# Unit 1's pairs 2 and 3 selected between the gram chunks of unit 0

## The chip, the cores and the metric

The kernel runs on one core of a Trainium2 chip. The metric is the device time of one execution in microseconds (us); lower is better. Three executions of the kernel before took 456.87, 457.18 and 457.71 us, median 457.18.

## What is computed

A recommendation tower over a batch of 2048 samples. Each sample looks up one 64-float row in each of 32 tables; all inner products of two different rows (496 of them), with 16 dense features behind them, go through three layers:

```python
e = jnp.stack([tbl_0[ids[:, 0]], ..., tbl_31[ids[:, 31]]], axis=1)   # 2048 x 32 x 64
gram = jnp.einsum('bnd,bmd->bnm', e, e)
z = gram[:, rows, cols]                                              # upper triangle
h = jnp.concatenate([z.reshape(2048, -1), dense_ctx], axis=1)        # 2048 x 512
h = jnp.maximum(h @ W_top1 + b_top1, 0.0)
h = jnp.maximum(h @ W_top2 + b_top2, 0.0)
y = h @ W_top3
```

All is in float32. Tables have 1000, 1250, 12500 or 125000 rows.

## The kernel before

The batch is cut into four units of 512 samples (u = 0 to 3). Each engine has one stream of instructions, written out by hand; streams meet at semaphores.

Twelve tables are *gathered*: GpSimd (POOL) issues an indirect DMA for 128 samples of one table (L272, 48 a unit), with 3 or 6 tiny memsets (L268) between two of them to pace them; the table `CLOSE` (L45) says for which numbers of a unit's 48 the pace is 3, and at the first number of that range POOL waits until TensorE has used a given piece of one-hots (L283, L284). TensorE transposes what came (L506, `turn`, three a round, two rounds r a unit) into `gat_ps`, and ScalarE (ACT) copies it to `vecs` (L314).

Twenty tables, in ten pairs g = 0 to 9, are *selected* by a matmul instead. The table lies in SBUF as three bf16 parts, 8 chunks of 125 rows (10 in pairs 7 to 9). VectorE (DVE) compares the ids of 512 samples, spread over all partitions in `ids_wide`, with row numbers (L443) and so makes one-hot columns; a pair has two halves of two pieces, and the ring `onehot` holds four pieces. `select(u, g, parts)` (L478 to L498) multiplies table parts with one-hots: 24 matmuls of 512 columns for half a pair of 8 chunks, 30 of 10 chunks. The two tables of a pair fill the upper and lower 64 partitions of one PSUM bank, `sel_ps[:, n % 2, :]`, where n numbers the pairs through all units. ACT empties it into `vecs` by four copies (`selected`, L301 to L308), and the next but one pair waits for that (L481).

The grams are matmuls of 64x32 on `vecs` (L521), in float32, recorded as two each. A unit has two rounds of four chunks; `gram(u, r, c)` is 128 recorded matmuls and 128 weight loads. Two chunks fill `gram_ps`, whose buffer b = 0 and b = 1 ACT (L323) and, for the last of a unit, DVE (L450) copy out before it is filled again (L516). `vecs` has room for one unit: ACT doesn't empty a pair of unit u + 1 before the last gram of unit u has ended (L403, L404).

SyncE then writes the grams to HBM (`rows_out`) and reads them back in the layout of the layers (`rows_back`), and TensorE does the layers of unit u - 1 between the grams of unit u, in the two banks of `tower_ps` (L537, L547, L556). At the grams of unit 0 there are no layers yet, and `tower_ps` isn't used.

TensorE's order around unit 0's grams (L572 to L586) is: half a pair 0 of unit 1, chunk (0,0,0), the other half, chunk (0,0,1), two turns, chunk (0,0,2), a turn, chunk (0,0,3), half of pair 1, chunk (0,1,0), the other half, chunks (0,1,1) to (0,1,3); then unit 1's pairs 2 to 9 (L564), each with both halves at once, and a turn behind each of the last three. DVE makes unit 1's one-hots in order, and copies the last grams of unit 0 behind those of pair 2 (L471, L472).

Of the kernel before, what the change touches and what calls it, by code (L numbers as in the profile page):

```python
# [17 lines left out]
HALF = UNIT // 2  # L18
# [23 lines left out]

SPACERS, WIDE_SPACERS = 3, 6

CLOSE = [range(0, 48), range(18, 46), range(22, 48), range(22, 48)]  # L45


def sel_no(u, g):
    return N_PAIRS * u + g
# [20 lines left out]
def dlrm_tower_kernel(nc, chunks, ctx_t, ids_gat, ids_sel, tables, packed, w1, b1, w2, b2, w3, out):  # L70
# [7 lines left out]
    with ExitStack() as ctx:  # L78
# [73 lines left out]
        y_full = sem("y_full")  # L152
        y_ready = sem("y_ready")
        y_out = [sem(f"y_out{b}") for b in range(2)]

        block = ctx.enter_context(nc.Block())

# [94 lines left out]
        @block.gpsimd  # L252
        def _(pool):
            nc.gpsimd.memset(ident[:], 0.0).then_inc(ident_zero, 1)
            for c, t in row_ids.items():
                nc.gpsimd.iota(t[:], pattern=[[1, c]], base=0, channel_multiplier=c,
                               allow_small_or_imprecise_dtypes=True).then_inc(row_ids_ready, 1)
            pool.wait_ge(ident_zero, 1)
            nc.gpsimd.affine_select(out=ident[:], in_=ident[:], compare_op=ALU.not_equal, fill=1.0, base=0,
                                    pattern=[[-1, P]], channel_multiplier=1).then_inc(ident_ready, 1)  # L260

            count = itertools.count()

            def spacer():
                n = next(count)
                if n > 0:
                    pool.wait_ge(spaced, n)
                nc.gpsimd.memset(spare[:], 0.0).then_inc(spaced, 1)  # L268

            def gather(u, r, x, k, h):  # L270
                at = ((u * ROUNDS + r) * 2 + h) * N_GAT + k
                nc.gpsimd.indirect_dma_start(  # L272
                    out=rows[:, r, k, h, :], out_offset=None, in_=tables[GATHERED[k]],
                    in_offset=bass.IndirectOffsetOnAxis(ap=gat_ids[:, at:at + 1], axis=0)).then_inc(rows_in[r][x], 16)

            for u in range(UNITS):
                if u < 2:
                    pool.wait_ge(gat_ids_in[u], 16)
                of_unit = [(r, x, k, h) for r in range(ROUNDS) for x in range(N_TURNS) for k in GROUPS[x] for h in range(2)]
                for n, (r, x, k, h) in enumerate(of_unit):  # L280
                    if u > 0 and k == GROUPS[x].start and h == 0:
                        pool.wait_ge(gat_full, gat_no(u - 1, r, x) + 1)
                    if n > 0 and n == CLOSE[u].start:  # L283
                        pool.wait_ge(onehot_used, piece_no(u, 2, 0, 1) + 1)  # L284
                    gather(u, r, x, k, h)
                    for _ in range(SPACERS if n in CLOSE[u] else WIDE_SPACERS):
                        spacer()

        @block.scalar
        def _(act):  # L290
# [10 lines left out]
            def selected(u, g):  # L301

                act.wait_ge(onehot_used, piece_no(u, g, 1, 1) + 1)
                for at in range(2):
                    for h in range(2):
                        last = nc.scalar.copy(vecs[DIM * h:DIM * h + DIM, :, N_GAT + 2 * g + at],  # L306
                                              sel_ps[DIM * at:DIM * at + DIM, sel_no(u, g) % 2, HALF * h:HALF * h + HALF])
                last.then_inc(sel_emptied, 1)  # L308

            def gathered(u, r, x):  # L310
# [105 lines left out]
        @block.vector  # L416
        def _(dve):
            dve.wait_ge(sel_ids_in, 16)
            nc.vector.tensor_copy(sel_f16[:], sel_ids[:]).then_inc(sel_f16_ready, 1)
            dve.wait_ge(row_ids_ready, len(row_ids))  # L420

            def rest(g):
                dve.wait_ge(hi_ready, g + 1)
                c0, k = pair_chunks[g]
                piece = stage[g % STAGE_SLOTS][:, 0:k, :]
                nc.vector.tensor_tensor(piece, piece, tabs[:, c0:c0 + k, 0, :], ALU.subtract).then_inc(rest_ready, 1)  # L426

            def low(g):
                dve.wait_ge(mid_ready, g + 1)
                c0, k = pair_chunks[g]  # L430
                nc.vector.tensor_tensor(tabs[:, c0:c0 + k, 2, :], stage[g % STAGE_SLOTS][:, 0:k, :],  # L431
                                        tabs[:, c0:c0 + k, 1, :], ALU.subtract).then_inc(tabs_ready, 1)

            def one_hots(u, g, half):
                if half == 0:
                    dve.wait_ge(wide_in[g], 16 * (u + 1))
                for at in range(2):
                    k, n = 2 * g + at, piece_no(u, g, half, at)
                    if n >= RING:
                        dve.wait_ge(onehot_used, n - RING + 1)  # L440
                    c0, c1 = halves[k][half]
                    for c in range(c0, c1):
                        last = nc.vector.tensor_scalar(onehot[:, n % RING, c - c0, :], ids_wide[:, k, :],  # L443
                                                       row_ids[chunks[k]][:, c:c + 1], None, ALU.is_equal)
                    last.then_inc(onehot_ready, 1)

            def gram(u, r, b, halves):
                dve.wait_ge(gram_full, emptied_no(u, r, b) + 1)
                for h in halves:
                    nc.vector.tensor_copy(gram_rows[:, r, h, :, 16 * b:16 * b + 16],  # L450
                                          gram_ps[:, h, :, :].rearrange("p i m -> p m i")).then_inc(gram_emptied, 1)

            rest(0)
            low(0)
            one_hots(0, 0, 0)
            rest(1)
            one_hots(0, 0, 1)
            low(1)
            rest(2)
            for g in range(1, N_PAIRS):  # L460
                one_hots(0, g, 0)
                if g + 1 < N_PAIRS:
                    low(g + 1)
                one_hots(0, g, 1)
                if g + 2 < N_PAIRS:
                    rest(g + 2)
            for u in range(1, UNITS):
                for g in range(N_PAIRS):
                    one_hots(u, g, 0)
                    one_hots(u, g, 1)  # L470
                    if g == 2:  # L471
                        gram(u - 1, 1, 1, (0, 1))  # L472
            for b in range(2):
                gram(LAST, 1, b, (1,))

        @block.tensor
        def _(pe):
            def select(u, g, parts=(0, 1)):  # L478
                n = sel_no(u, g)
                if n >= 2 and parts[0] == 0:  # L480
                    pe.wait_ge(sel_emptied, n - 1)  # L481
                if u == 0:
                    pe.wait_ge(tabs_ready, g + 1)
                last = [None, None]
                for half in parts:
                    pe.wait_ge(onehot_ready, piece_no(u, g, half, 1) + 1)
                    c0, c1 = halves[2 * g][half]
                    for c in range(c0, c1):
                        for part in range(PARTS):
                            for at in range(2):  # L490
                                k = 2 * g + at
                                last[at] = nc.tensor.matmul(  # L492
                                    sel_ps[DIM * at:DIM * at + DIM, n % 2, :], tabs[:, first_chunk[k] + c, part, :],
                                    onehot[:, piece_no(u, g, half, at) % RING, c - c0, :],
                                    start=(c == 0 and part == 0), stop=(c == chunks[k] - 1 and part == PARTS - 1),
                                    skip_group_check=True)
                    for at in range(2):
                        last[at].then_inc(onehot_used, 1)  # L498
# [62 lines left out]
            select(0, 1)  # L561
            pe.wait_ge(ident_ready, 1)
            for u in range(UNITS):
                for g in range(2, N_PAIRS):  # L564
                    select(u, g)
                    if g == 2 and u > 1:
                        layer3(u - 2)
# [1 line left out]
                        turn(u, 0, g - N_PAIRS + N_TURNS)  # L569
                if u == 0:  # L570

                    select(1, 0, (0,))  # L572
                    gram(0, 0, 0)
                    select(1, 0, (1,))
                    gram(0, 0, 1)
                    turn(0, 1, 0)
                    turn(0, 1, 1)
                    gram(0, 0, 2)
                    for x in range(2, N_TURNS):
                        turn(0, 1, x)  # L580
                    gram(0, 0, 3)
                    select(1, 1, (0,))
                    gram(0, 1, 0)
                    select(1, 1, (1,))
                    for c in range(1, CHUNKS):
                        gram(0, 1, c)  # L586
                    pe.wait_ge(w_in, 16 * 5)
                elif u < LAST:
# [94 lines left out]
```

## Time and profile before

| | |
|---|---|
| median of three executions | 457.18 us |
| profiled execution | 458.73 us |
| its span, first to last instruction | 456.9 us |
| TensorE matmul (PE) busy | 396.5 us, 87% |
| VectorE (DVE) busy | 231.5 us, 51% |
| ScalarE (ACT) busy | 166.6 us, 36% |
| GpSimd (POOL) busy | 303.5 us, 66% |
| mean granted TensorE clock | 0.978 |

Start times in rows are microseconds from the start of the span. An end of a matmul is modelled, so that two groups in a row overlap by some 0.07 us; distances are best taken from start to start. "issue" as the releaser of an idle time means that nothing else in the profile explains it. The granted clock is a share of 2.4 GHz: 1.00 is 2.4 GHz and 0.50 is 1.2 GHz.

### The profile page before, as it was taken

How to read it: one execution, taken by the hardware profiler on the slowest of the kernel's cores; microseconds unless marked ns; L12 is line 12 of the kernel's file. 1: busy time of each engine (PE TensorE's matmuls, PEld its weight loads, DVE VectorE, ACT ScalarE, POOL GpSimd, SP SyncE). 2: the span in 40 equal slices, each digit the busy share in tenths (PEclk: the TensorE clock that was granted, in tenths of full speed). 3: DMA queues.
4: the chain of work that ended last, by engine and by line, in shares of the span. 5: the costliest groups of instructions: out<-in, count | busy, mean ns of one | idle time of the engine just before them, and what ended most of it. 6: DMA issues, size and time to landing. Idle time of an engine off the chain costs nothing.

```text
span 456.9 us, 15285 instructions
## 1 busy us (share of the span) xinstructions
PE 396.5 (87%) x6516; PEld 224.8 (49%) x6516; DVE 231.5 (51%) x717; ACT 166.6 (36%) x264; POOL 303.5 (66%) x968
## 2 busy tenths in 40 slices
PE   0777788978679999789889999979999999888998
PEld 0343344554445555445544655445554655454476
DVE  2999999732239887004327897203517896000000
ACT  3346755511044435122144443312154433421222
POOL 6888889887848898778738888778608886000000
PEclk9999999997769999999999999999999999999999
DMA  5944912101056921100037832010027510024610
GB/s 179 379 129 110 322 43 61 45 19 22 18 101 128 252 64 45 20 20 16 19 51 157 236 81 65 19 21 18 14 43 151 117 23 19 3 31 78 118 51 0
DMA packets 38238, 37.53 MB, mean 82 GB/s; under 512 B 13781, under 2 KB 26903, under 8 KB 38042
## 3 DMA queue, kind: packets, MB, share of 16 engines
q1 hardware_dynamic: 31594, 29.04, 25.4%
q0 software_dynamic: 6144, 6.30, 6.7%
q10 hardware_dynamic: 432, 1.21, 0.8%
q8 instruction: 51, 0.84, 0.8%
q14 instruction: 17, 0.14, 0.1%
HBM read 28.45 MB, written 8.09 MB: 80 GB/s over the span
## 4 chain that ended last, share of the span: by engine, by line
PE 75%; DVE 12%; issue 7%; ACT 3%; DMA 2%; ACTq 0%
PE sel_ps L492 42%; PE tower_ps L537 12%; PE gram_ps L521 12%; DVE onehot L443 8%; PE tower_ps L547 5%; PE gat_ps L506 2%; DVE tabs L431 2%; ACT vecs L306 2%; DVE work L426 2%; PE tower_ps L556 2%; DMA ids_wide<-ids_scratch 1%; DMA ids_scratch<-sel_f 1%; ACT work L323 1%; DMA sel_ids<-in_ids_sel_dram 1%; ACT tabs L299 0%
## 5 line engine op out<-in xcount | busy, mean ns | idle before, releaser
L492 PE MATMUL sel_ps<-onehot,tabs 128*64 128x512 bf16 x2064 | 237.6, 387 | 32.3 <-DVE onehot L443 15.1
L443 DVE TENSOR_SCALAR onehot<-ids_wide,row_ids 128x512 bf16<-128x512 f16 x688 | 202.7, 366 | 123.7 <-PE sel_ps L492 115.1
L272 POOL DMA_INDIRECT rows<-in_tbl_dram,gat_ids x192 | 195.3, 1017 | 48.0 <-PE sel_ps L492 26.2
L492 PEld LDWEIGHTS sel_ps<-onehot,tabs 128*64 128x64 bf16 x2064 | 125.3, 112 | 139.0 <-issue 40.1
L306 ACT COPY vecs<-sel_ps 64x256 f32<-64x256 f32 x160 | 96.9, 605 | 112.2 <-PE sel_ps L492 69.3
L268 POOL MEMSET spare<- 128x1 f32 x768 | 107.8, 140 | 33.2
L521 PE MATMUL gram_ps<-vecs 64*32 64x32 f32 x4096 | 54.3, 204 | 24.9 <-issue 22.6
L521 PEld LDWEIGHTS gram_ps<-vecs 64*32 64x32 f32 x4096 | 44.9, 108 | 50.0 <-issue 45.6
L537 PE MATMUL tower_ps<-work,w_sb 128*128 128x512 f32 (+1 forms) x160 | 59.3, 515 | 0.5 <-issue 0.5
L537 PEld LDWEIGHTS tower_ps<-work,w_sb 128*128 128x128 f32 x160 | 29.0, 190 | 19.0 <-issue 17.0
L450 DVE COPY work<-gram_ps 128x512 f32<-128x512 f32 x8 | 5.3, 688 | 61.5 <-PE gram_ps L521 61.5
L323 ACT COPY work<-gram_ps 128x512 f32<-128x512 f32 x24 | 13.0, 589 | 55.0 <-PE gram_ps L521 55.0
L329 ACT ACTIVATE h<-tower_ps,b_sb 128x512 f32<-128x512 f32 (+1 forms) x20 | 12.0, 602 | 57.1 <-PE tower_ps L537 57.1
L547 PE MATMUL tower_ps<-h,w_sb 128*128 128x512 f32 (+1 forms) x80 | 29.7, 516 | 0.0
L299 ACT CAST tabs<-work 128x1024 bf16<-128x1024 f32 (+1 forms) x10 | 11.1, 1109 | 25.3 <-DVE work L426 19.6
L547 PEld LDWEIGHTS tower_ps<-h,w_sb 128*128 128x128 f32 x80 | 14.6, 190 | 9.2 <-issue 8.1
L314 ACT COPY vecs<-gat_ps 128x512 f32<-128x512 f32 x24 | 13.8, 594 | 13.2 <-PE gat_ps L506 12.9
L506 PE MATMUL gat_ps<-ident,rows 128*128 128x128 f32 x96 | 14.9, 284 | 0.8 <-ACT vecs L314 0.8
L426 DVE TENSOR_TENSOR work<-work,tabs 128x1024 f32<-128x1024 f32 (+1 forms) x10 | 12.9, 1292 | 2.5 <-ACT tabs L294 2.5
L506 PEld LDWEIGHTS gat_ps<-ident,rows 128*128 128x128 f32 x96 | 10.1, 140 | 7.0 <-issue 5.8
L431 DVE TENSOR_TENSOR tabs<-work,tabs 128x1024 bf16<-128x1024 f32 (+1 forms) x10 | 12.9, 1294 | 1.1 <-ACT tabs L299 1.1
L294 ACT CAST tabs<-work 128x1024 bf16<-128x1024 f32 (+1 forms) x10 | 11.1, 1108 | 5.3 <-DMA work<-in_packed_dram 5.1
(13 smaller groups left out, 20.3 us busy)
## 6 DMA issues: line engine op xcount, KB each, us to landing
ids_wide<-ids_scratch SPq DMA_DIRECT2D x40, 256.0 KB
rows<-in_tbl_dram,gat_ids POOLq DMA_INDIRECT x192
products<-work SPq DMA_DIRECT2D x12, 248.0 KB
products<-work SPq DMA_DIRECT2D x24, 120.0 KB
work<-in_packed_dram SPq DMA_DIRECT2D x5, 512.0 KB
work<-products SPq DMA_DIRECT2D x9, 256.0 KB
work<-in_packed_dram SPq DMA_DIRECT2D x3, 640.0 KB
work<-in_packed_dram ACTq DMA_DIRECT2D x2, 512.0 KB
```

The lines of the kernel that those rows point to most:

```text
L268: nc.gpsimd.memset(spare[:], 0.0).then_inc(spaced, 1)
L272: nc.gpsimd.indirect_dma_start(out=rows[:, r, k, h, :], out_offset=None, in_=tables[GATHERED[k]], in_offset=bass.IndirectOffsetOnAxis(ap=g ...
L306: last = nc.scalar.copy(vecs[DIM * h:DIM * h + DIM, :, N_GAT + 2 * g + at], sel_ps[DIM * at:DIM * at + DIM, sel_no(u, g) % 2, HALF * h:HAL ...
L323: nc.scalar.copy(gram_rows[:, r, h, :, 16 * b:16 * b + 16], gram_ps[:, h, :, :].rearrange("p i m -> p m i")).then_inc(gram_emptied, 1)
L426: nc.vector.tensor_tensor(piece, piece, tabs[:, c0:c0 + k, 0, :], ALU.subtract).then_inc(rest_ready, 1)
L431: nc.vector.tensor_tensor(tabs[:, c0:c0 + k, 2, :], stage[g % STAGE_SLOTS][:, 0:k, :], tabs[:, c0:c0 + k, 1, :], ALU.subtract).then_inc(ta ...
L443: last = nc.vector.tensor_scalar(onehot[:, n % RING, c - c0, :], ids_wide[:, k, :], row_ids[chunks[k]][:, c:c + 1], None, ALU.is_equal)
L492: last[at] = nc.tensor.matmul(sel_ps[DIM * at:DIM * at + DIM, n % 2, :], tabs[:, first_chunk[k] + c, part, :], onehot[:, piece_no(u, g, ha ...
L506: last = nc.tensor.transpose(gat_ps[:, n % 2, P * at:P * at + P], rows[:, r, k, :, :].rearrange("p h d -> p (h d)"), ident[:])
L521: last = nc.tensor.matmul(gram_ps[32 * s:32 * s + 32, h, i, :], v, v, start=True, stop=True, skip_group_check=True)
L537: last = nc.tensor.matmul(tower_ps[:, (v + j) % 2, 0:width], w1_sb[:, c, P * j:P * j + P], z[:, c, x0:x0 + width], start=(c == 0), stop=(c ...
L547: last = nc.tensor.matmul(tower_ps[:, (v + o) % 2, 0:width], w2_sb[:, j, P * o:P * o + P], h1[:, j, 0:width], start=(j == 0), stop=(j == J ...
```

## The change

Pairs 2 and 3 of unit 1 are put into the two banks of `tower_ps` and moved in front of the chunks of round 1. TensorE's order at unit 0's grams becomes eight times half a pair (pairs 0 to 3 of unit 1) and a chunk, with two turns in front of the third half and one in front of the fourth; the loop of unit 1 then begins with pair 4. The waits of `select` follow: pairs 2 and 3 wait for no emptying, and pairs 4 and 5 for that of pairs 0 and 1, which is what pairs 2 and 3 waited for. DVE copies the last grams of unit 0 between the two halves of pair 4's one-hots. `CLOSE` changes for units 1 to 3, and POOL's wait in unit 1 is for pair 4 instead of pair 2.

```diff
-CLOSE = [range(0, 48), range(18, 46), range(22, 48), range(22, 48)]
+CLOSE = [range(0, 48), range(18, 42), range(17, 45), range(20, 48)]
@@
+        def sel_bank(u, g):
+
+            return tower_ps[:, g - 2, :] if u == 1 and g in (2, 3) else sel_ps[:, sel_no(u, g) % 2, :]
@@ POOL
-                        pool.wait_ge(onehot_used, piece_no(u, 2, 0, 1) + 1)
+                        pool.wait_ge(onehot_used, piece_no(u, 4 if u == 1 else 2, 0, 1) + 1)
@@ ACT, selected
-                                              sel_ps[DIM * at:DIM * at + DIM, sel_no(u, g) % 2, HALF * h:HALF * h + HALF])
+                                              sel_bank(u, g)[DIM * at:DIM * at + DIM, HALF * h:HALF * h + HALF])
@@ DVE
                     one_hots(u, g, 0)
+                    if u == 1 and g == 4:
+                        gram(0, 1, 1, (0, 1))
                     one_hots(u, g, 1)
-                    if g == 2:
+                    if u > 1 and g == 2:
                         gram(u - 1, 1, 1, (0, 1))
@@ TensorE, select
-                if n >= 2 and parts[0] == 0:
+                if u == 1 and g in (4, 5) and parts[0] == 0:
+                    pe.wait_ge(sel_emptied, n - 3)
+                elif n >= 2 and parts[0] == 0 and not (u == 1 and g in (2, 3)):
                     pe.wait_ge(sel_emptied, n - 1)
@@
-                                    sel_ps[DIM * at:DIM * at + DIM, n % 2, :], tabs[:, first_chunk[k] + c, part, :],
+                                    sel_bank(u, g)[DIM * at:DIM * at + DIM, :], tabs[:, first_chunk[k] + c, part, :],
@@ TensorE, order
-                for g in range(2, N_PAIRS):
+                for g in range(4 if u == 1 else 2, N_PAIRS):
@@
-                    select(1, 0, (0,))
-                    gram(0, 0, 0)
-                    select(1, 0, (1,))
-                    gram(0, 0, 1)
-                    turn(0, 1, 0)
-                    turn(0, 1, 1)
-                    gram(0, 0, 2)
-                    for x in range(2, N_TURNS):
-                        turn(0, 1, x)
-                    gram(0, 0, 3)
-                    select(1, 1, (0,))
-                    gram(0, 1, 0)
-                    select(1, 1, (1,))
-                    for c in range(1, CHUNKS):
+                    for c in range(CHUNKS):
+                        if c == 2:
+                            turn(0, 1, 0)
+                            turn(0, 1, 1)
+                        if c == 3:
+                            turn(0, 1, 2)
+                        select(1, c // 2, (c % 2,))
+                        gram(0, 0, c)
+                    for c in range(CHUNKS):
+                        select(1, 2 + c // 2, (c % 2,))
                         gram(0, 1, c)
```

## Rows read from the trace of the kernel before

**Rows 1.** The page: the chain that ended last, shares by engine.
```profile
PE 75%; DVE 12%; issue 7%; ACT 3%; DMA 2%; ACTq 0%
```

**Rows 2.** Stretches: PE, PEld, DVE, ACT, POOL busy, granted clock, DMA share, GB/s.
```profile
110.00:120.00 10.00, 7.53 (x357) 5.00 (x353) 4.73 (x16) 1.07 (x2) 8.30 (x33) 1.00 0.09 16
...
150.00:160.00 10.00, 9.51 (x88) 5.74 (x86) 9.08 (x32) 4.28 (x8) 8.95 (x25) 1.00 0.88 253
```

**Rows 3.** Timeline of TensorE: start, length, what, idle before. Unit 0's grams.
```profile
92.85 2.78 PE L492 MATMUL sel_ps<-onehot,tabs 128*64 128x512 bf16 x24
...
97.29 1.09 PE L506 MATMUL gat_ps<-ident,rows 128*128 128x128 f32 x8
...
101.63 0.66 PE L506 MATMUL gat_ps<-ident,rows 128*128 128x128 f32 x4
...
106.40 4.50 PE L492 MATMUL sel_ps<-onehot,tabs 128*64 128x512 bf16 x24
...
113.39 2.78 PE L492 MATMUL sel_ps<-onehot,tabs 128*64 128x512 bf16 x24
...
117.25 0.94 PE L521 MATMUL gram_ps<-vecs 64*32 64x32 f32 x84 [0.45 <-issue]
...
119.36 1.11 PE L521 MATMUL gram_ps<-vecs 64*32 64x32 f32 x90 [1.17 <-ACT work L323]
```

**Rows 4.** Timeline of TensorE behind unit 0's grams.
```profile
128.52 18.60 PE L492 MATMUL sel_ps<-onehot,tabs 128*64 128x512 bf16 x144 [2.49 <-issue]
147.38 10.71 PE L492 MATMUL sel_ps<-onehot,tabs 128*64 128x512 bf16 x96 [0.26 <-issue]
...
180.03 3.60 PE L537 MATMUL tower_ps<-work,w_sb 128*128 128x512 f32 x8
```

**Rows 5.** Stretches of one us: TensorE busy, granted clock, DMA share, GB/s.
```profile
103.00:104.00 1.00, 0.97 (x51) 0.51 0.18 33
...
120.00:121.00 1.00, 0.47 (x45) 0.54 0.17 33
...
133.00:134.00 1.00, 1.00 (x8) 0.63 0.81 141
...
404.00:405.00 1.00, 0.32 (x37) 1.00 0.00 0
```

**Rows 6.** Timeline of TensorE: half pairs and chunks of units 1 and 2.
```profile
213.79 2.78 PE L492 MATMUL sel_ps<-onehot,tabs 128*64 128x512 bf16 x24
...
218.28 2.78 PE L492 MATMUL sel_ps<-onehot,tabs 128*64 128x512 bf16 x24
...
223.56 3.70 PE L547 MATMUL tower_ps<-h,w_sb 128*128 128x512 f32 x8
...
319.25 2.78 PE L492 MATMUL sel_ps<-onehot,tabs 128*64 128x512 bf16 x24
...
323.62 2.78 PE L492 MATMUL sel_ps<-onehot,tabs 128*64 128x512 bf16 x24
...
328.16 3.70 PE L547 MATMUL tower_ps<-h,w_sb 128*128 128x512 f32 x8
```

**Rows 7.** Timeline of TensorE: a chunk of unit 1 between two parts of layer 1.
```profile
203.44 0.69 PE L521 MATMUL gram_ps<-vecs 64*32 64x32 f32 x44
...
206.88 1.09 PE L506 MATMUL gat_ps<-ident,rows 128*128 128x128 f32 x8
```

**Rows 8.** Timelines of ACT, DVE, POOL and SyncE's queue behind unit 0's grams.
```profile
126.06 4.74 ACT L306 COPY vecs<-sel_ps 64x256 f32<-64x256 f32 x8 [6.76 <-PE gram_ps L521]
126.07 1.29 DVE L450 COPY work<-gram_ps 128x512 f32<-128x512 f32 x2 [7.46 <-PE gram_ps L521]
...
133.93 2.33 DVE L443 TENSOR_SCALAR onehot<-ids_wide,row_ids 128x512 bf16<-128x512 f16 x8 [6.57 <-PE sel_ps L492]
...
134.13 0.97 POOL L272 DMA_INDIRECT rows<-in_tbl_dram,gat_ids  x1 [5.85 <-PE sel_ps L492]
...
148.34 0.43 SPq L201 DMA_DIRECT2D work<-products  x1
```

## The prediction

> **What bounds the kernel now.** I began with the page's chain of waits, by engine. The reader should see that three quarters of the span are TensorE [rows 1], so a change counts only by what it does to TensorE's stream. Then came TensorE's timeline at unit 0's grams, which is read by start-to-start distances. Half a pair takes 2.7 us, and it is followed by a chunk. From 92.85 to 97.29 a half and a chunk together take 4.44 us; from 113.39 to 118.19 (the end of the chunk's last piece, 117.25 + 0.94) 4.80 us [rows 3]. Chunks with another chunk or turns in front are dearer. From 97.29 to 106.40 lie three turns and two chunks: 9.11 us, of which the turns are 1.09 + 0.66 us, so a chunk costs 3.7 us. The last two chunks run from 119.36 [rows 3] to 126.06, where ACT is released [rows 8]: 3.35 us each, and 1.17 us of waiting for ACT lie ahead of them. The idle times inside the chunks have no releaser but "issue". Between such pauses 90 matmuls run in 1.11 us [rows 3]. So a chunk is not limited by the array; it is limited by how fast instructions reach it, and a chunk behind long matmuls has part of its instructions waiting in TensorE's queue already.
>
> The granted clock gives the second loss. It falls to 0.50 (1.2 GHz) in the us from 103, and again in the us from 120, both times when nothing but chunks, turns and idle time had come since the last half pair; it is back in the us from 133 [rows 5]. The half pair at 106.40 takes 4.50 us where the others take 2.78 [rows 3].
>
> The third loss is the wait behind the last chunk: TensorE idles until 128.52 [rows 4], since pair 2 needs the bank of pair 0, and ACT may empty that only when unit 0's last gram has ended; its eight copies for two pairs take 4.74 us, so one pair 2.4 us [rows 8].
>
> **The change part by part.** Up to 97.29 both kernels issue the same.
>
> *Eight halves before eight chunks.* From 97.29 come three turns, 1.09 + 0.66 = 1.75 us [rows 3], and six times a half with a chunk. This combination at full clock is seen six times apart from the first: 4.44 and 4.80 [rows 3], and in units 1 and 2 213.79 to 218.28 = 4.49, 218.28 to 223.56 = 5.28, 319.25 to 323.62 = 4.37, 323.62 to 328.16 = 4.54 [rows 6]. The mean is 27.92 / 6 = 4.65 us. So the last gram ends at 97.29 + 1.75 + 27.9 = 126.9, and not at 126.06: 0.9 us later, with 96 more matmuls done. Lower bound: all at 4.37, 125.3. Upper bound: all at 5.28, 130.7. I take the mean, since half of the six lie within 0.15 us of it.
>
> *The wait behind the grams stays.* Pair 4 needs pair 0's bank as pair 2 did, so TensorE waits 2.5 us again and starts pair 4 at 126.9 + 2.5 = 129.4.
>
> *Where the old kernel stands at the same point.* Its pairs 2, 3 and 4 are the 144 matmuls from 128.52, ending at 147.12; a pair at full clock is 5.36 us, half of the 10.71 us of 96 matmuls [rows 4]. It begins pair 4 at 147.12 - 5.36 = 141.8. The gain is 141.8 - 129.4 = **12.4 us**. In other terms: 1.7 us for the half pair at 1.2 GHz, 2.6 us for the time from 128.52 to 133.7 at 1.2 GHz (half of 5.2), and 8.1 us of issue time and of the wait for ACT that long matmuls now cover.
>
> *The other bank.* No row shows a selection into `tower_ps`. Layers write it, 8 recorded matmuls in 3.70 us [rows 6] with no idle time ahead that the bank caused, and ACT empties it behind them; I take 0. As bounds: a gain is excluded, as nothing gets shorter; the loss is at most what an ordinary wait for ACT costs here, 1.2 us [rows 3].
>
> *ACT's copies.* Four pairs now wait for the last gram. At 2.4 to 2.5 us a pair ACT is through at 126.9 + 9.9 = 136.8 and through with pair 4 at 139.3. Pair 6 needs that at 129.4 + 2 x 5.36 = 140.1. The cover is 0.8 us; gone, it costs up to 1 us once, as ACT is twice as fast per pair as TensorE. ACT's program is otherwise unmoved, so the layers' copies aren't queued behind anything new.
>
> *DVE's copy of the last grams* sits between the halves of pair 4's one-hots. Behind it is queued the second half: 126.9 + 1.29 + 2.4 = 130.6 [rows 8], wanted at 129.4 + 2.7 = 132.1. The next half starts when the first of pair 4 is used, 132.1, and is there at 134.5, wanted at 134.8. During the grams DVE makes a half in 2.33 us [rows 8], of the 4.65 that TensorE needs. Cost 0; if the cover of 0.3 us is gone, some tenths, as in the old trace, whose idle 0.26 us ahead of 147.38 [rows 4] is of this kind.
>
> *SyncE* sends unit 0's grams out when both copies are done, now 0.9 us later, and then reads them back; the last read was issued at 148.34 [rows 8], and the DMA engines were 0.88 busy from 150 to 160 [rows 2]. Layer 1 started at 180.03 [rows 4] and will want the data at 167.7. With the issue at 149.2 that leaves 18 us. Cost 0; the bounds are below as a rival. The loads of `ids_wide` behind it wait for one-hots, which come earlier too.
>
> *POOL.* Its gather 18 of unit 1 waited until 134.13 for pair 2 [rows 8] and now waits for pair 4's first half, 129.4 + 2.7 = 132.1: 2 us earlier, while TensorE is 12.4 us ahead. The last turns of unit 1 come at some 201; 30 gathers, each 1.0 us [rows 8] and at most as much again for its memsets, end by 192 at most. `CLOSE` keeps the dense gathers to the stretch without layers. Cost and gain both within 0.5 us, taken as 0.
>
> From there on all is moved as a whole. The profiled execution, 458.73 us with its span of 456.9, becomes 446.3, and as it lies 1.6 us above the median of 457.18, the median becomes **444.8 us**.
>
> **A rule of the notes, weighed.** 90 of a chunk's matmuls in 1.11 us [rows 3] are 12 ns each. The Trainium skill, "TensorE: Matmul & The Clock Gate", section "Wait — 56ns, not 53.3ns?", says that matmuls never start closer than about 25 ns, however small. By that a chunk would be 3.2 us whatever stands in front of it. The trace disagrees; but chunks of about that length exist here, and so the matter is a rival, below, with its own rows.
>
> **Rivals.**
> - *The clock falls once more, in the wait behind the last chunk.* For: from the end of the last half pair to pair 4 lie a chunk (about 1.9 us) and 2.5 us of idleness, 4.4 us without long matmuls, and the fall in the us from 120 came some 4 us after the half pair from 113.39. Against: in unit 3, in the us from 404, TensorE is 0.32 busy between two parts of a layer, and the clock stays at 1.00 [rows 5]; a fall so late hits little. Price: 1.7 us (one half pair at 4.50 for 2.78) to 2.6 us (the second time). Result 446.5 to 447.4, say 447.1.
> - *A chunk has its own price.* In unit 1 the chunk from 203.44 to 206.88 takes 3.44 us [rows 7] though 3.6 us of layer 1 stand ahead of it. If chunks cost 3.2 us here, each of the six pairs is 2.7 + 3.2 = 5.9 us, 1.25 more than taken, together 7.5: 452.3. Against: no chunk behind a half pair at full clock took over 2.6 us.
> - *The products come back late.* If rows written 0.9 us later landed only at 175, layer 1 would start 7.3 us after TensorE is ready: 452.1; landing as late as 180 leaves nothing. Against: the DMA share of the ten us from 150 [rows 2] is the reading back itself.
> - *Slower than before.* The clock goes to 1.2 GHz at 103 as it did and never gets back between the halves, since chunks leave TensorE idle now and then. Then six halves cost 1.72 more, 10.3 us, the six chunks about 0.4 more, 2.4, and pair 4 2.6: 444.8 + 15.3 = 460.1. It decides if half of a stretch isn't enough to keep the clock. Against: from 110 to 120 TensorE did a chunk, a half pair and a chunk, 7.53 us busy of ten, and the clock stayed at 1.00 [rows 2].
>
> **How the numbers follow.** The forecast has 0.56, the clock's fall behind the grams 0.27, the chunk's own price 0.07, late products 0.04, slower 0.03, and something not seen that eats the gain 0.03. The lower end is the six combinations at 4.37: 444.8 - 1.7 = 443.1, rounded to 442.8. Upwards the combinations at 5.28 give 448.6, and a fall of the clock with combinations a little above the mean 450; the rivals at 452 and above stay out. A difference under 0.2% (0.9 us) can't be told from none here. Faster by more: 0.94; within: 0.02; slower: 0.04.
>
> **What will show it.** In the trace of the changed kernel: six half-and-chunk distances of 4.4 to 5.3 us and a last gram near 127; the clock at 1.00 from 97 to 127; an idle time of 2.5 us with ACT as its cause ahead of pair 4, at 129.4; the first part of layer 1 at 167.7 with no idle time ahead; and from there the same distances as before. I am wrong if the distances are near 6, if the clock is at 0.50 for longer than 5 us, or if an idle time stands ahead of layer 1 or pair 6.

## The result and the profile after

The changed kernel took 451.75 us (median of 454.50, 450.27, 453.06 and 450.44) against 457.44 us; the ratio is 0.9871, with a 95% interval of 0.9835 to 0.9907. It is 5.7 us faster where 12.4 were forecast, and outside the range by 1.75 us. Its profiled execution is the slowest of the four, 454.5 us with a span of 452.7, against 458.73 and 456.9 before.

At the change itself the timeline of TensorE answers to [rows 3] and [rows 4] as follows (start, length, what, idle time before it).

```profile
97.39 1.09 PE L514 MATMUL gat_ps<-ident,rows 128*128 128x128 f32 x8
98.41 2.78 PE L500 MATMUL sel_ps<-onehot,tabs 128*64 128x512 bf16 x24
...
104.30 2.78 PE L500 MATMUL sel_ps<-onehot,tabs 128*64 128x512 bf16 x24
...
108.29 2.78 PE L500 MATMUL tower_ps<-onehot,tabs 128*64 128x512 bf16 x24
...
112.66 2.78 PE L500 MATMUL tower_ps<-onehot,tabs 128*64 128x512 bf16 x24
...
117.18 2.78 PE L500 MATMUL tower_ps<-onehot,tabs 128*64 128x512 bf16 x24
...
121.64 2.78 PE L500 MATMUL tower_ps<-onehot,tabs 128*64 128x512 bf16 x24
...
127.28 0.35 PE L529 MATMUL gram_ps<-vecs 64*32 64x32 f32 x12 [0.48 <-issue]
130.15 17.74 PE L500 MATMUL sel_ps<-onehot,tabs 128*64 128x512 bf16 x144 [2.52 <-issue]
148.67 6.67 PE L500 MATMUL sel_ps<-onehot,tabs 128*64 128x512 bf16 x60 [0.78 <-DVE onehot L447]
...
170.12 3.60 PE L545 MATMUL tower_ps<-work,w_sb 128*128 128x512 f32 x8
```

The rows show six halves; each with its chunk takes 3.99 to 5.99 us. A half of a pair in `tower_ps` takes as long as one in `sel_ps` (2.78 us). The last gram ends at 127.63, the idle 2.5 us stayed, and layer 1 begins at 170.12 with nothing ahead of it. Against [rows 4] (180.03) the lead there is 9.9 us. The 144 matmuls of pairs 4 to 6 take 17.74 us where 16.1 would be full speed (three times 5.36).

Behind that point the rows of layer 1 and of the turns in units 1 and 2 tell where the lead went.

```profile
184.69 5.40 PE L545 MATMUL tower_ps<-work,w_sb 128*128 128x512 f32 x8
...
192.64 3.70 PE L545 MATMUL tower_ps<-work,w_sb 128*128 128x512 f32 x8
...
280.81 1.35 PE L529 MATMUL gram_ps<-vecs 64*32 64x32 f32 x112
...
283.66 5.40 PE L545 MATMUL tower_ps<-work,w_sb 128*128 128x512 f32 x8
...
301.37 0.64 PE L529 MATMUL gram_ps<-vecs 64*32 64x32 f32 x50
...
305.45 1.97 PE L514 MATMUL gat_ps<-ident,rows 128*128 128x128 f32 x8
307.35 7.27 PE L500 MATMUL sel_ps<-onehot,tabs 128*64 128x512 bf16 x48
...
386.78 1.88 PE L545 MATMUL tower_ps<-work,w_sb 128*128 128x512 f32 x4
```

The last of them, layer 1 at the grams of unit 3, stood in the kernel before at:

```profile
389.79 1.88 PE L537 MATMUL tower_ps<-work,w_sb 128*128 128x512 f32 x4
```

So the lead of 9.9 us is down to 3.0 there. And the stretches of 2 us (length, TensorE busy, granted clock, DMA share, GB/s) show what the clock did.

```profile
184.00:186.00 2.00, 1.54 (x8) 0.74 0.07 16
...
284.00:286.00 2.00, 2.00 (x3) 0.50 0.09 15
...
306.00:308.00 2.00, 2.00 (x11) 0.50 0.08 16
```

Three times in units 1 and 2 the clock goes to 1.2 GHz. A part of layer 1 takes 5.40 us instead of 3.70, twice; in the third stretch two turns take 1.97 instead of 1.09 and the next pair (48 matmuls) 7.27 instead of 5.37. That is 1.7 + 1.7 + 0.9 + 1.9 = 6.2 us, and 9.9 - 6.2 = 3.7; the span is 4.2 us shorter. Up to unit 3 the lead shrinks by 6.9 us, so the falls are most of it. Single chunks are up to 1.5 us longer or shorter than in the kernel before, which nearly cancels, and one half, at 319.07, takes 3.39 us at full clock. In the profile of the kernel before the clock is never below 1.00 in these units.

### The profile page after: what moved, and what is told of

Same layout as the page of the kernel before. It is cut to its first block, busy times and chain, and to the rows that moved or that the text cites. A ratio compares the mean times of both kernels' runs of the same rounds, so it can differ in the third digit from the quotient of the medians.

```text
span 452.7 us, 15283 instructions
## 1 busy us (share of the span) xinstructions
PE 398.1 (88%) x6516; PEld 223.7 (49%) x6516; DVE 230.6 (51%) x717; ACT 166.9 (37%) x264; POOL 304.6 (67%) x968
## 4 chain that ended last, share of the span: by engine, by line
PE 75%; DVE 14%; issue 6%; ACT 3%; DMA 2%; DVEq 0%
PE sel_ps L500 38%; PE tower_ps L545 13%; PE gram_ps L529 11%; DVE onehot L447 10%; PE tower_ps L555 6%; PE gat_ps L514 3%; PE tower_ps L500 2%; DVE tabs L435 2%; ACT vecs L310 2%; DVE work L430 2%; PE tower_ps L564 2%; DMA ids_wide<-ids_scratch 1%; DMA ids_scratch<-sel_f 1%; DMA sel_ids<-in_ids_sel_dram 1%; ACT tabs L303 0%
## 5 line engine op out<-in xcount | busy, mean ns | idle before, releaser
L500 PE MATMUL sel_ps<-onehot,tabs 128*64 128x512 bf16 x1968 | 226.7, 386 | 32.4 <-DVE onehot L447 16.7
L500 PEld LDWEIGHTS sel_ps<-onehot,tabs 128*64 128x64 bf16 x1968 | 118.8, 111 | 135.0 <-issue 39.7
L272 POOL MEMSET spare<- 128x1 f32 x768 | 109.1, 142 | 33.2
L310 ACT COPY vecs<-sel_ps 64x256 f32<-64x256 f32 x152 | 92.1, 606 | 103.1 <-PE sel_ps L500 60.1
L529 PE MATMUL gram_ps<-vecs 64*32 64x32 f32 x4096 | 51.8, 201 | 19.5 <-issue 18.6
L529 PEld LDWEIGHTS gram_ps<-vecs 64*32 64x32 f32 x4096 | 43.3, 105 | 44.7 <-issue 42.0
L545 PE MATMUL tower_ps<-work,w_sb 128*128 128x512 f32 (+1 forms) x160 | 62.8, 539 | 0.0
L545 PEld LDWEIGHTS tower_ps<-work,w_sb 128*128 128x128 f32 x160 | 30.1, 197 | 20.9 <-issue 18.8
```

Of the source, the lines that this page charges most:

```text
L500: last[at] = nc.tensor.matmul(sel_bank(u, g)[DIM * at:DIM * at + DIM, :], tabs[:, first_chunk[k] + c, part, :], onehot[:, piece_no(u, g, h ...
L529: last = nc.tensor.matmul(gram_ps[32 * s:32 * s + 32, h, i, :], v, v, start=True, stop=True, skip_group_check=True)
L545: last = nc.tensor.matmul(tower_ps[:, (v + j) % 2, 0:width], w1_sb[:, c, P * j:P * j + P], z[:, c, x0:x0 + width], start=(c == 0), stop=(c ...
```

## Experiments

The sessions differ. In some, a chunk behind a part of layer 1 takes 2.5 to 4.4 us; I call that slow feed. In others it takes 1.2 to 1.8; fast feed. The name is a reading: the pauses in the chunks have no releaser but "issue". It is no fixed trait of a chip: the chip with number 1 showed fast feed in one session and slow feed in another. The expectations, written as this came out, speak of chips of a first kind (slow feed) and of a second (fast feed). Every kernel is compared with the kernel before in its own session.

| kernel | time | before | ratio (95%) | feed |
|---|---|---|---|---|
| changed (first result) | 451.75 | 457.44 | 0.9871 (0.9835 to 0.9907) | slow |
| fill22 | 433.17 | 439.42 | 0.9859 (0.9827 to 0.9890) | fast |
| shift15 | 434.09 | 439.42 | 0.9892 (0.9853 to 0.9931) | fast |
| close_old | 432.70 | 439.42 | 0.9858 (0.9825 to 0.9892) | fast |
| split | 435.58 | 439.42 | 0.9921 (0.9886 to 0.9956) | fast |
| after_again (changed) | 432.00 | 438.53 | 0.9848 (0.9817 to 0.9878) | fast |
| before_again | 438.96 | 438.53 | 1.0013 (0.9992 to 1.0034) | fast |
| before_shift15 | 442.03 | 438.53 | 1.0085 (1.0058 to 1.0113) | fast |
| before_split | 442.34 | 438.53 | 1.0083 (1.0057 to 1.0108) | fast |
| before_slow | 496.69 | 456.76 | 1.0847 (1.0787 to 1.0908) | slow |
| after_slow | 493.99 | 456.76 | 1.0794 (1.0727 to 1.0861) | slow |
| gat_bank | 447.98 | 456.76 | 0.9805 (0.9753 to 0.9857) | slow |
| round0 | 457.11 | 456.76 | 0.9996 (0.9964 to 1.0028) | slow |
| after3 (changed) | 430.15 | 437.83 | 0.9845 (0.9804 to 0.9886) | fast |
| before3 | 438.76 | 437.83 | 1.0014 (0.9989 to 1.0039) | fast |
| gat_bank2 | 426.54 | 437.83 | 0.9740 (0.9717 to 0.9764) | fast |
| split2 | 436.45 | 437.83 | 0.9963 (0.9938 to 0.9987) | fast |
| after4 (changed) | 450.74 | 455.82 | 0.9893 (0.9863 to 0.9923) | slow |
| gat_bank3 | 446.36 | 455.82 | 0.9801 (0.9769 to 0.9832) | slow |

**fill22: something to do in the wait**

```diff
                     pe.wait_ge(w_in, 16 * 5)
+                    filler(22)
```

> The changed kernel with 22 matmuls of half a pair's shape, whose result nobody uses, put behind unit 0's last gram, where TensorE otherwise idles 2.5 us for ACT. Theory 1 (the lead is eaten by falls of the clock): the fall at 130 goes, layer 1 of unit 0 starts 1.7 us earlier than 170.1, at 168.4; the total is 1.7 us less if the later falls stay, and anything from 446 to 452 if they move. Theory 2 (the lead is eaten by gathers and DMA, through the new pace of POOL): layer 1 at 168.4 and the total back at what it was, 450 to 453, with the clock as it was in units 1 and 2.

The 22 matmuls are 64 x 512 and go into the first bank of `gat_ps`, where nobody reads them.

The fall behind the grams went: pairs 4 to 6 took 16.08 us and layer 1 began at 167.32, 1.8 us before close_old's 169.12 in that session. The total was no better: 433.17 us against close_old's 432.70. Its profile has a pause of 1.40 us ahead of 204.41 and a fall of the clock there, where a part of layer 2 takes 5.39 us for 3.70, and the layer parts from 211 to 223 come 1.8 to 1.9 us later than in close_old. So the local part was right, and in the profiled execution the 1.8 us and as much again were lost in the next unit. But the fall isn't the whole reason: two of the four executions have a mean clock of 1.000, so no fall, and took 432.63 and 432.93 us, no less than close_old's two at 0.996 (431.45 and 432.41). What eats the gain there isn't shown; the changed kernel itself wasn't run in that session.

**shift15 and before_shift15: everything later by 1.7 us**

```diff
+                    if u == 1 and g == 5:
+                        filler(15)
                     select(u, g)
```

> The changed kernel with 15 unused matmuls (1.7 us at full clock) in front of pair 5 of unit 1: everything behind comes 1.7 us later, nothing else differs. Theory 1: the falls of the clock in units 1 and 2 depend on when a chunk comes, so they are others than before; the total differs from +1.7 us by over 1.5 us in either direction (it may even fall to 449). Theory 2 or a fixed cost: 1.7 us more than the changed kernel, 453.4, with the falls moved along by 1.7 us.

> The kernel before with 15 unused matmuls (1.7 us at full clock) in front of pair 5 of unit 1. Theory 1: the time moves by something else than 1.7 us, as the falls of the clock move: 437 to 443. A fixed cost: 441.1.

shift15 was 1.4 us above close_old in its session, which doesn't tell the theories apart; before_shift15 was 3.5 us above the kernel before, twice the 1.7 put in. So in the second case the shift is not passed on one to one; the profiles, of one execution each, don't show why. Inconclusive.

**close_old: POOL's pace as before**

```diff
-CLOSE = [range(0, 48), range(18, 42), range(17, 45), range(20, 48)]
+CLOSE = [range(0, 48), range(18, 46), range(22, 48), range(22, 48)]
```

> The changed kernel with the table CLOSE of the kernel before, so POOL's pace is as before (its wait in unit 1 stays at pair 4). Theory 1: as the changed kernel, 450 to 454. Theory 2 (the new pace costs the lead): 445 to 447.

The ratio, 0.9858, is that of the changed kernel with fast feed (0.9848, 0.9845). With fast feed the pace table is worth nothing either way, and theory 2 is out there. With slow feed, where the lead was lost, it wasn't run.

**after_again and before_again: both kernels, one session**

> The changed kernel unaltered, on the chip of the experiments so far, where the kernel before took 439.4 us instead of 457.4. There the other kernels' chunks behind long matmuls took 1.3 to 1.8 us. Theory 4 (the size of the gain depends on how fast instructions reach TensorE on the chip at hand): the kernel before gains less from interleaving here; the changed one takes 433 to 435 us, a gain of 4.5 to 6 us. Theory 1 alone (clock falls ate it): the changed kernel's runs with a mean clock of 0.996 and above are 10 us or more ahead of the kernel before.

> The kernel before, profiled on this chip. Theory 4: chunks between two parts of layer 1 take 1.3 to 1.9 us instead of 2.6 to 3.9, in all units, which is most of the 18 us between the two chips; chunks behind chunks take about 2.5 instead of 3.3. Theory 1 alone: the same chunk times as on the first chip and only fewer falls of the clock (at most 5 us of the 18).

The rows of unit 1 in before_again, which answer to [rows 7]:

```profile
184.15 1.85 PE L521 MATMUL gram_ps<-vecs 64*32 64x32 f32 x128
185.92 3.70 PE L537 MATMUL tower_ps<-work,w_sb 128*128 128x512 f32 x8
189.56 1.29 PE L521 MATMUL gram_ps<-vecs 64*32 64x32 f32 x128
190.78 3.70 PE L537 MATMUL tower_ps<-work,w_sb 128*128 128x512 f32 x8
```

The chunks are 1.29 to 1.85 us with no pause in them. The kernel's gram rows (busy time, mean, idle time ahead), the first of the kernel before's own profile, the second of before_again, tell the same: TensorE idled 22.6 us of "issue" ahead of grams in the whole span with slow feed, and 9.2 here.

```profile
L521 PE MATMUL gram_ps<-vecs 64*32 64x32 f32 x4096 | 54.3, 204 | 24.9 <-issue 22.6 <-ACT work L323 1.4 <-ACT vecs L306 0.9
...
L521 PE MATMUL gram_ps<-vecs 64*32 64x32 f32 x4096 | 47.2, 202 | 12.2 <-issue 9.2 <-ACT work L323 1.4 <-ACT vecs L306 0.9
```

Busy and idle time of these rows together are 79.2 and 59.4 us; the difference of 19.8 is nearly all of the 20.4 us between the two spans.

The change gains 6.5 us here, a little over the 4.5 to 6 expected, and it keeps it: layer 1 begins at 169.48 against 175.71 (6.2 us), and the spans are 430.1 and 436.5 (6.4 us). Neither profile has a fall in units 1 and 2. So there is a smaller lead, nothing of it lost, and no smaller gain in the end (6.5 us; 5.7 with slow feed). The changed kernel still has the fall behind the grams: 18.69 us for the 144 matmuls, 2.6 too many.

**split, before_split, split2: half chunks between half parts of layer 1**

```diff
-                        layer1(u - 1, c)
-                        gram(u, 0, c)
+                        for part in range(2):
+                            layer1(u - 1, c, (part,))
+                            gram(u, 0, c, (part,))
```

> The changed kernel with each part of layer 1 and each chunk of round 0 of units 1 and 2 cut in two and alternated (half a layer part, half a chunk, twice). Theory 1: TensorE is never long without heavy matmuls there, the clock stays at 1.00 in units 1 and 2; and with a full queue ahead of each half chunk the distance from one layer part to the next falls from 6.6 us to 5.3, eight times: 438 to 443. Theory 3 (a chunk has a time of its own): the distances stay, and at most the falls go: 446 to 449.

> The kernel before with layer 1 and the chunks of round 0 of units 1 and 2 cut in halves and alternated. Theory 4: on this chip there is little left to gain, as whole chunks are fed fast already: 437 to 440. Theory 1: it keeps the clock up in units 1 and 2: 435 to 437.

> The changed kernel with layer 1 and the chunks of round 0 of units 1 and 2 cut in halves and alternated, on the same chip as the changed kernel. On a chip of the first kind, if slow feeding and the falls in it cost there: 3 to 8 us faster than the changed kernel, no fall between 165 and 200. On one of the second kind: 2 to 4 us slower, since a half chunk takes 0.7 us more than half of a whole one and there is nothing to save.

All three missed or were worse than hoped: split is 2.9 us slower than close_old in its session, before_split 3.8 us slower than the kernel before, split2 6.3 us slower than the changed kernel (after3). In split, the stretch from the first part of layer 1 to the turns behind the last chunk is 169.60 to 191.72, 22.1 us, where after_again needs 169.48 to 189.87, 20.4. The first half chunk waits 0.93 us for ACT, which half a part no longer hides, and a half chunk takes 0.76 us and up. All three sessions had fast feed, so what splitting does with slow feed was not seen.

**before_slow and after_slow: feeding made slower by hand**

```diff
                     for h in range(2):
+                        pe.wait_ge(ident_ready, 1)
+                        pe.wait_ge(tabs_ready, 1)
                         for s in range(Q):
```

> The kernel before with two waits that are long fulfilled ahead of every four gram matmuls (16 times a chunk): the same work, but instructions reach TensorE more slowly, as on the first chip. Theory 5 (slow feeding of the chunks makes stretches with few matmuls, in which the clock falls, and the place of the falls is a lottery): chunks between parts of layer 1 take 2.5 us or more, the time rises by over 8 us, and falls of the clock appear outside unit 0's grams. Rival (the first chip is slower for another reason, such as DMA): the time rises only by what the waits cost, all clocks as before.

> The changed kernel with the same waits in its chunks. Theory 5: with chunks as dear as on the first chip the local lead at layer 1 of unit 0 is some 10 us, more than the 6.2 us of this chip, and part of it is lost or not by falls of the clock in units 1 and 2: 4 to 11 us faster than before_slow, with runs that scatter by over 2 us. Rival: 6.5 us faster, as without the waits.

The waits cost far more than meant: 39.9 us. In before_slow's profile the granted clock is below 1.00 in seven places from 195 us on, of which two stand here (columns as in the stretches above); the kernel before's own profile has none there. Its mean fell to 0.942.

```profile
196.00:198.00 2.00, 2.00 (x4) 0.50 0.10 16
...
354.00:356.00 2.00, 2.00 (x4) 0.50 0.00 0
```

So starving TensorE of gram instructions does bring the clock down in later units, for either kernel. The change was worth 2.7 us, and its lead at layer 1 was 4.9 us (182.56 against 187.48); theory 5 gave 10 for the lead and 4 to 11 for the total, and missed both. One reading, not tested, is that waits inside a chunk are not covered by long matmuls ahead of it. At this size the waits are no copy of slow feed.

**round0: half of the change**

```diff
+                    for c in range(CHUNKS):        # turns as in the changed kernel
+                        select(1, c // 2, (c % 2,))
+                        gram(0, 0, c)
+                    for c in range(CHUNKS):
+                        gram(0, 1, c)
```

> Half of the change: the four halves of pairs 0 and 1 ahead of the four chunks of round 0, as in the changed kernel; round 1's four chunks follow each other, and pairs 2 and 3 come behind ACT's wait as before. By my prediction each half moved covers its part, so about half of the gain. By the trace of the kernel before on this chip, chunks in a row with no long matmuls lose the clock: four in a row then lose more than the three before did, and the time is that of the kernel before, 437 to 440. So the gain hangs on pairs 2 and 3 and their banks.

457.11 against 456.76: nothing. Its timeline shows why. Round 1's chunks wait for ACT's copies (1.98 and 2.42 us), the clock falls at 112 and stays down to 133, and the wait ahead of pair 2 is there.

```profile
110.35 0.58 PE L521 MATMUL gram_ps<-vecs 64*32 64x32 f32 x45 [1.98 <-ACT work L323]
...
119.08 1.70 PE L521 MATMUL gram_ps<-vecs 64*32 64x32 f32 x118 [2.42 <-ACT work L323]
...
128.39 18.17 PE L492 MATMUL sel_ps<-onehot,tabs 128*64 128x512 bf16 x144 [3.75 <-issue]
```

So four halves in other places gain nothing; the gain comes with eight halves for eight chunks, for which the two more banks are needed.

**gat_bank, gat_bank2, gat_bank3: pair 4 in a third bank**

```diff
+            if u == 1 and g == 4:
+                return gat_ps[:, 0, :]
@@ DVE
-                    if u == 1 and g == 4:
-                        gram(0, 1, 1, (0, 1))
                     one_hots(u, g, 1)
+                    if u == 1 and g == 4:
+                        gram(0, 1, 1, (0, 1))
@@ TensorE: pair 4 waits for nothing, pair 6 for the emptying of pair 0
+                elif u == 1 and g == 6 and parts[0] == 0:
+                    pe.wait_ge(sel_emptied, n - 5)
@@ turn(1, 0, 0)
+                    pe.wait_ge(sel_emptied, sel_no(1, 4) + 1)
```

> The changed kernel, and unit 1's pair 4 selected into a bank of gat_ps, which nobody uses then; so TensorE needn't wait for ACT behind unit 0's last gram (DVE makes both halves of pair 4's one-hots ahead of its copy). If the wait and the fall of the clock in it are what is left to gain there: no idle 2.5 us, no fall at 130, layer 1 of unit 0 4 to 5 us earlier than 169.5, and 427 to 428.5 in all. If the kernel gives such leads back later: 430 to 432.

> Pair 4 in a bank of gat_ps, on the same chip as the changed kernel. It takes away the idle 2.5 us and the fall of the clock in it (1.7 to 2.6 us): 3.5 to 5 us faster than the changed kernel if nothing gives it back.

> Pair 4 in a bank of gat_ps, on the same chip as after4. On a chip of the first kind 3.5 to 5 us faster than the changed kernel, as the wait and the fall in it cost the same 1.2 GHz half pairs there; on one of the second kind 3.6 us again.

The rows of gat_bank2 behind unit 0's grams:

```profile
126.04 5.37 PE L506 MATMUL gat_ps<-onehot,tabs 128*64 128x512 bf16 x48
131.41 10.72 PE L506 MATMUL sel_ps<-onehot,tabs 128*64 128x512 bf16 x96
...
164.34 3.60 PE L553 MATMUL tower_ps<-work,w_sb 128*128 128x512 f32 x8
```

No idle 2.5 us and no fall: layer 1 begins at 164.34, 4.2 us before after3's 168.52. The five executions all have a mean clock of 1.000, and the time is 3.6 us below the changed kernel's in that session, 11.3 below the kernel before's. With slow feed gat_bank3 is 4.4 us below after4, though both profiles with slow feed (gat_bank, gat_bank3) have a fall at 172 and one at 298. The 3.5 to 5 us expected of gat_bank2 and gat_bank3 came. This is the fastest version found, 2.6% and 2.0% below the kernel before.

**after3, before3 and after4: the changed kernel again**

> The changed kernel unaltered, once more, with its rivals on one chip. Two kinds of chip have been seen: before at 457 (chunks fed slowly) and at 439. If the gain is made by the same mechanism on both, it is 5 to 7 us on either. On a chip of the first kind the lead at the first part of layer 1 should be some 10 us against before3 and the profile should show where the rest goes: falls of the clock in units 1 and 2, each in a chunk of over 2.5 us between two parts of layer 1. On one of the second kind: lead 6 us there and at the end.

> The kernel before, profiled on the same chip as after3. On a chip of the first kind, if falls of the clock in units 1 and 2 are a lottery for both kernels, this profile may show one too; if only the changed kernel has them, something in its pace brings them about.

> The changed kernel once more. On a chip of the first kind (kernel before at 457): 450 to 454, chunks of units 1 and 2 between parts of layer 1 of 2.5 us and more, and where the profile has falls of the clock in units 1 and 2 the lead falls at those places and nowhere else. On one of the second kind (438): 430 to 433.

after3 and before3 repeat the fast feed: 7.7 us gained, layer 1 at 168.52 against 177.04, a lead of 8.5 us there and of 8.7 at the end (spans 428.8 and 437.5). The lead differs from after_again's 6.2 on both sides: before3 comes 1.3 us later than before_again (its clock is below 1.00 from 117 to 131, in before_again from 122 to 130), and after3 1.0 us earlier than after_again (its 144 matmuls take 17.74 us, not 18.69). after4 brought slow feed, and its profiled execution, 448.44 us, is the fastest of all ten with slow feed. Its rows for what the first profile had at 184.69 and 283.66:

```profile
184.47 3.70 PE L545 MATMUL tower_ps<-work,w_sb 128*128 128x512 f32 x8
...
283.14 3.70 PE L545 MATMUL tower_ps<-work,w_sb 128*128 128x512 f32 x8
```

Its first part of layer 1 begins at 170.66, its clock is below 1.00 only behind the grams, and its span is 446.6. Against the profile of the kernel before that is a lead of 9.4 us at layer 1 [rows 4] and of 10.3 at the end. It isn't the gain of a typical execution: that profile (458.73 us) is a slow one of its kernel, and in after4's own session the kernel before had a median of 455.82 and a lowest of 453.86, so that the gain was 5.1 us by medians and 5.4 between the two fastest. The ten executions of the changed kernel with slow feed, by their mean clock:

| mean clock | times |
|---|---|
| 0.996 | 448.44 |
| 0.992 | 449.96, 450.27, 450.41, 450.44 |
| 0.989 | 451.07, 451.40, 452.40 |
| 0.985 | 453.06 |
| 0.981 | 454.50 |

Each further step down costs about 1.5 us (454.50 - 448.44 over four steps). Other kernels are less orderly: gat_bank's three executions at 0.992 took 445.07, 447.27 and 448.84 us.

## Why the prediction was wrong

**Eight halves before eight chunks: right.** The last gram was forecast at 126.9 and ended at 127.63. The six distances had a mean of (127.63 - 97.39 - 1.02 - 0.55) / 6 = 4.8 us, taken as 4.65. The other bank cost nothing, as taken. [rows 6] were good rows for the mean, but not for single chunks: the last, from 124.35 to 127.63, took 3.3 us, with its half 5.99, above the bound of 5.28.

**The clock in the wait behind the grams: wrong, and it was a rival.** I gave 0.27 to a fall there. All four profiles of the changed kernel have it, with either feed. It cost 17.74 - 16.1 = 1.7 us in the first and 2.6 in after_again. The forecast put it at nothing in the sum, against the us from 404 [rows 5], where TensorE was 0.32 busy; but that is a chunk between a part of a layer and turns. Here came a chunk of 3.3 us, taken as 1.9, and then 2.5 us of idle time. With the grams 0.7 us late this is all of the shortfall at layer 1, 170.12 for 167.7. gat_bank, which removes both, shows the wait with the fall to be worth 3.6 and 4.4 us in all.

**"From there on all is moved as a whole": this step failed.** The lead of 9.9 us at layer 1 became 4.2 at the end of the first profile. 6.2 us of it lie in three stretches at 1.2 GHz in units 1 and 2. That the falls carry the loss is shown by these rows and by after4: same kernel, same feed, no such fall, and 10.3 us of lead over the same profile at the end. With fast feed, where no profile of the changed kernel has a fall in units 1 and 2, the step held: 6.2 us became 6.4, and 8.5 became 8.7. The middle two of the ten executions with slow feed, 450.44 and 451.07 us, have mean clocks of 0.992 and 0.989, one and two steps below after4's profile.

What is left open: the forecast of 444.8, with 1.7 for the fall behind the grams and 0.7 for the later grams, gives 447.2, and after4's profile, which has just that fall, took 448.44. So 1.2 us aren't accounted for, and more against after4's own session, in which the kernel before was faster by 1.6 us. By the table, one more step would put the changed kernel without any fall at about 446.9; this is an extrapolation, not a run, and fill22's executions at 1.000 show that taking a fall away need not pay.

**What brings the falls about is shown in part.** They come at a chunk with pauses in it: 3.85, 2.85 and 4.08 us at the falls of 184, 284 and 305, the last of them partly at 1.2 GHz itself. In after_again, after3 and gat_bank2, where chunks there take at most 1.8 us, there is none in units 1 and 2, and with the added waits there are many. fill22 has one with fast feed, behind a chunk with 1.40 us of idle time. But [rows 7] has such a chunk, 3.44 us, with no fall behind it. Which of the long chunks the clock falls behind differs between profiles of one kernel (three falls in the first, none in after4) and stays open, and so does why the changed kernel's first profile had three and the kernel before's none. The new pace of POOL wasn't tried with slow feed, so that it has a part in this isn't ruled out. The kernel before scatters as well, from 452.6 to 459.4 us with slow feed.

**How far the rows carry.** I took the pauses in chunks as a property of the kernel. They are in part one of the session: 18 us between 457 and 439 for the same kernel. With fast feed the lead at layer 1 is smaller, 6.2 and 8.5 us instead of 9.9. The gain in the end is not: 6.5 and 7.7 us with fast feed, 5.7 and 5.1 with slow feed. What makes feed fast or slow wasn't found; the packets of the larger instruction queue (51, 0.84 MB) are the same in the kernel before's profile and in before_again.

**ACT, DVE, SyncE and POOL: right in the sum.** No idle time stood ahead of pair 6 or of layer 1. DVE's one-hots for pair 7 came 0.78 us late (148.67). The kernel before had idled as long between its pairs 4 and 7, 0.26 and 0.49 us, so this cost nothing more.

**The rivals.** A chunk with its own price is out: the chunk behind the half from 104.30 is over in 1.3 us. That is 10 ns for each of the 128 recorded matmuls. The Trainium skill's floor of about 25 ns between starts ("TensorE: Matmul & The Clock Gate", "Wait — 56ns, not 53.3ns?") doesn't hold for these matmuls, which write four groups of 32 output partitions in turn; by the floor, an estimate, it would have been 3.2 us. Products too late is out. The slower case needed the clock to fall between the halves; it stayed at 1.00 from 97 to 130.

## What to carry to other kernels

A gain upstream is not simply passed on when the clock hangs on what TensorE does: look in every later stage for chunks of small matmuls with pauses in them, and widen the range by what a fall costs in each (1.7 to 2.8 us here). Before moving work in front of a wait, ask for another free bank and take the wait away too. And profile the kernel before in more than one session before taking its pauses for its own; one profile can be a slow execution of its kernel, as 458.73 was.

## What the runs showed of the hardware

The same kernel had two levels, near 457 and near 439 us, and nearly all of the difference (19.8 of 20.4 us between two profiles) lies in the busy time and the pauses of the 64x32 matmuls with their weight loads: chunks of 128 behind a part of layer 1 took 2.5 to 4.4 us or 1.2 to 1.8. That instructions reach TensorE more slowly is the likely reason and not shown. Two fulfilled waits ahead of every four matmuls, 512 pairs in all, cost 39.9 us (before_slow), 78 ns a pair with the falls of the clock that they brought. And the clock went to 1.2 GHz though TensorE had not been idle for longer than 1.2 us in that stretch: in the kernel before it was 0.75, 0.19 and 0.64 busy in the three us from 117, all with such small matmuls, and the fall came in the next.
